# Expert feed-forward on one Trainium2 core: the low-input products of the last 64 features as two 64-row matmuls

## The chip, the cores and the metric

The kernel runs on one core of one Trainium2 chip. The metric is the device time in microseconds (us) of one execution, the median of several; a change is read against that median.

## The reference, cut to what matters

An image tokenizer and text tokens give 32 sequences of 164 tokens of width 192. An attention-like block follows, and then the part that this change touches, a feed-forward layer with 8 experts of width 384, of which each token uses 2:

```python
xn = _rms_norm(layernorm(h), norm_w)
xf = xn.reshape(-1, D)                      # D = 192
logits = xf @ router_w.T
probs = softmax(logits); _, top_idx = top_k(probs, 2)
g = einsum('td,efd->tef', xf, gate_w)       # 8 experts, 384 wide
u = einsum('td,efd->tef', xf, up_w)
h = silu(g) * u * comb_w[:, :, None]
y = einsum('tef,edf->td', h, down_w)
```

All is float32. The kernel reaches that accuracy with a faster matmul format: a value is split into a high part, which the format holds, and a low part, the remainder. A product of two values is then the sum of high by high, high by low and low by high.

## The kernel before, in words

The tokens are sorted by expert into tiles of 128 rows in DRAM (`disp`). The last stage works through 89 such tiles, called slots (`SLOTS = 89`), in a software pipeline with two of each buffer. Step k of the pipeline does on TensorE, in this order: "x", the two transposes of slot k+2 (L941); "g", gate's and up's matmuls of slot k+1 (L952 to L956); "h", the three transposes of the hidden tile of slot k (L963); "t", the six matmuls of the down projection of slot k-1 (L972, L974). ScalarE makes the high parts (`xh`, `hth`), the SiLU and a copy; VectorE makes the low parts (`xl`, `htl`), the product of gate and up (`hh`), and the sum of the result tile (`ysb`). GpSimd copies the 128 destination rows of the slot (`dnow`, L687) and issues the indirect DMA that scatters the result (L690). SP loads the next slot's rows (L428 to L431).

The weights stay in SBUF in `wa`, 128 partitions, per expert three blocks (r = 0, 1, 2) of 384 columns for gate and 384 for up. Block 0 holds the high parts of features 0 to 127, block 1 their low parts. Block 2, called rest, holds features 128 to 191, the high parts in partitions 0 to 63 and the low parts in partitions 64 to 127. The inputs `xh` and `xl` hold these 64 features twice, in both halves of their second 128 columns, so one 128-row matmul with rest gives the product with the high and the low part of the weight together. Each of gate and up therefore takes five matmuls of 128 rows by 384 columns: L952 (xh by high), L953 (xh by low), L954 (xl by high), L955 (xh by rest), L956 (xl by rest). The expert of a slot is read from a table (`tab`) into a register, and `wa` is addressed by that register. All ten matmuls end with one semaphore increment, on which ScalarE waits for the SiLU.

Earlier in the kernel, between patch tokens and the attention block, `text_kv` (L752) and `head_kv` (L760) issue pairs of float32 matmuls of 64 rows, one of partitions 0 to 63, the next of partitions 64 to 127, into different PSUM banks. A float32 matmul call there leaves two records in the trace, one after the other.

The weights' low parts are made on VectorE by `low`, in units spread over the attention loop; the low part of rest is made in partitions 64 to 127 for gate and for up.

Of the kernel before, what the change touches and what calls it, by code (L numbers as in the profile page):

```python
# [10 lines left out]
F32R = mybir.dt.float32r  # L11
# [4 lines left out]
P = 128  # L16
# [19 lines left out]
NE = 8  # L36
DE = 384
FC = DE // P
REGION = TILES * P + P
SLOTS = TILES * 2 + NE - 1  # L40
# [34 lines left out]
UNITS = DOWN_UNITS + 3 * NE  # L75
RING = 3
# [2 lines left out]
LN_GROUPS = (range(9, 17), range(17, 25), range(25, 33), range(33, 41), EARLY, LATE)  # L79
NORMED = tuple(t for g in LN_GROUPS for t in g)  # L80
XBUF = 3
TURNS = 2 * CHUNKS


# [23 lines left out]
def build(nc, pixels, bands, text, W, bias, attn_w, par, norm_w, router_w, gu_w, down_w, consts, out):  # L108
    with ExitStack() as ctx:
# [4 lines left out]
        def at(name, shape, dt, offset):  # L114
            return nc.alloc_sbuf_tensor_at(name, shape, dt, offset=offset)
# [13 lines left out]
        def sem(name):  # L129
            return ctx.enter_context(nc.semaphore(name))  # L130
# [5 lines left out]
        r_gh = room(2 * 2 * NH * D * 4)  # L136
# [16 lines left out]
        wa = at("wa", [P, NE * 3 * 2 * DE], F32R, r_w)  # L153
        wa5 = wa[:].rearrange("p (e r w f) -> p e r w f", e=NE, r=3, w=2)
        wd = at("wd", [P, NE * FC * 2 * D], F32R, r_wd)
        wd4 = wd[:].rearrange("p (g h d) -> p g h d", h=2, d=D)
        ring = [at(f"ring{i}", [P, DE], F32, r_gh + 18688 + 1536 * i) for i in range(RING)]
# [18 lines left out]
        xl = [at(f"xl{i}", [P, 2 * P], F32R, r_ffn + 2048 + 1024 * i) for i in range(2)]  # L176
# [3 lines left out]
        htl = [at(f"htl{i}", [P, DE], F32R, r_ffn + 13312 + 1536 * i) for i in range(2)]  # L180
        ysb = [at(f"ysb{i}", [P, D], F32, r_ffn + 16384 + 768 * i) for i in range(2)]
        ylo = [at(f"ylo{i}", [P, D], F32, r_ffn + 17920 + 768 * i) for i in range(2)]

        yall = at("yall", [P, TILES * 2 * D], F32, r_w)

# [2 lines left out]
        tab = sb("tab", [P, 2, TAB], I32)  # L188
# [19 lines left out]
        nwab = qpar[:, Q_NORM:Q_GB]  # L208
# [45 lines left out]
        bank = [ctx.enter_context(nc.psum_tensor(f"bank{i}", [P, 512], F32)) for i in range(5)]  # L254
# [38 lines left out]
        s_hi, s_lo, s_cnt = sem("expert_high"), sem("expert_low"), sem("counts_ready")  # L293
        s_cread, s_tab, s_zf = sem("counts_mm"), sem("table"), sem("tail_zeroed")
# [3 lines left out]
            "xsT_mm", "xsT_high", "xsT_low", "gate_up_mm", "silu", "hidden"))  # L298
        s_ht, s_hth, s_htl, s_dn, s_y = (sem(n) for n in (
            "hiddenT_mm", "hiddenT_high", "hiddenT_low", "down_mm", "y_ready"))  # L300
        s_ylo = sem("down_low_out")
        s_exp, s_w, s_dest, s_dnow = (sem(n) for n in (
            "softmax_exp", "weights_ready", "result_rows", "result_rows_copied"))
        s_yg = [sem(f"results_in{i}") for i in range(len(LOADS) - 1)]
# [353 lines left out]
        @block.gpsimd  # L658
        def _(pool):
            pool.memset(onesf[:], 1.0).then_inc(s_pool, 1)  # L660
            pool.memset(ident[:], 0.0).then_inc(s_pool, 1)
            pool.memset(onesb[:], 1.0).then_inc(s_pool, 1)
            pool.memset(ltri[:], 1.0).then_inc(s_pool, 1)
            pool.wait_ge(s_pool, 4)
            pool.affine_select(out=ident[:], in_=ident[:], compare_op=ALU.not_equal, fill=1.0, base=0,
                               pattern=[[-1, P]], channel_multiplier=1)

            pool.affine_select(out=ltri[:], in_=ltri[:], compare_op=ALU.is_gt, fill=0.0, base=0,
                               pattern=[[1, P]], channel_multiplier=-1).then_inc(s_cons, 1)


            def scatter(c):
                pool.wait_ge(s_pos, c + 1)
                for j in range(nt(c)):
                    pool.wait_ge(s_xf, 4 * c + j + 1)
                    pool.nop(nofuse=True)
                    for k in range(2):
                        pool.indirect_dma_start(disp, bass.IndirectOffsetOnAxis(  # L678
                            ap=posu[c % XBUF][:, 2 * j + k:2 * j + k + 1], axis=0), xfd[c % XBUF][:, j, :], None
                            ).then_inc(s_scat[c % XBUF][j], 16)  # L680

            for c in range(CHUNKS):
                scatter(c)

            def store(k, b):
                pool.wait_ge(s_y, k + 1)
                pool.tensor_copy(dnow[b][:], dest[:, bass.ds(k, 1)]).then_inc(s_dnow, 1)  # L687
                pool.wait_ge(s_dnow, k + 1)
                pool.nop(nofuse=True)
                pool.indirect_dma_start(ydram, bass.IndirectOffsetOnAxis(ap=dnow[b][:], axis=0),  # L690
                                        ysb[b][:], None).then_inc(s_ys[b], 16)

            with pool.Fori(0, SLOTS // 2) as i:
                for b in range(2):
                    store(2 * i + b, b)
            if SLOTS % 2:
                store(SLOTS - 1, 0)

        @block.tensor
        def _(pe):  # L700
# [232 lines left out]
            def step(k, b, parts="xght"):  # L933

                if "x" in parts:

                    pe.wait_ge(s_xs[b], 16 * (k - b + 4))
                    if not isinstance(k, int) or k >= -1:
                        pe.wait_ge(s_xlo, k + 2)
                    for m in range(2):  # L940
                        ins = pe.transpose(bank[5][:, P * m:P * m + P], xs[b][:, P * m:P * m + P], ident[:])  # L941
                    ins.then_inc(s_xst, 1)
                if "g" in parts:
                    o = 1 - b
                    e = pe.snap(gate_reg[o], min_val=0, max_val=NE - 1)
                    pe.wait_ge(s_xlo, k + 2)


                    for which in range(2):
                        high, low, rest = (wa[:, bass.ds(e * (6 * DE) + 2 * DE * r + DE * which, DE)] for r in range(3))  # L950
                        acc = bank[2 * o + which][:, 0:DE]
                        pe.matmul(acc, xh[o][:, 0:P], high, start=True, stop=False)  # L952
                        pe.matmul(acc, xh[o][:, 0:P], low, start=False, stop=False)  # L953
                        pe.matmul(acc, xl[o][:, 0:P], high, start=False, stop=False)  # L954
                        pe.matmul(acc, xh[o][:, P:2 * P], rest, start=False, stop=False)  # L955
                        ins = pe.matmul(acc, xl[o][:, P:2 * P], rest, start=False, stop=True)  # L956
                    ins.then_inc(s_gu, 1)
                if "h" in parts:
                    pe.wait_ge(s_hh, k + 1)
                    if not isinstance(k, int) or k >= 1:  # L960
                        pe.wait_ge(s_htl, k)
                    for c in range(FC):
                        ins = pe.transpose(bank[4][:, P * c:P * c + P], hh[b][:, P * c:P * c + P], ident[:])  # L963
                    ins.then_inc(s_ht, 1)
                if "t" in parts:
                    o = 1 - b
                    e = pe.snap(down_reg[o], min_val=0, max_val=NE - 1)
                    pe.wait_ge(s_htl, k)
                    for c in range(FC):
                        both = bass.ds(e * (FC * 2 * D) + c * 2 * D, 2 * D)  # L970
                        high = bass.ds(e * (FC * 2 * D) + c * 2 * D, D)
                        pe.matmul(bank[6 + o][:, 0:2 * D], hth[o][:, P * c:P * c + P], wd[:, both],  # L972
                                  start=(c == 0), stop=False)
                        ins = pe.matmul(bank[6 + o][:, 0:D], htl[o][:, P * c:P * c + P], wd[:, high],  # L974
                                        start=False, stop=(c == FC - 1))
                    ins.then_inc(s_dn, 1)
                if "g" in parts:
                    pe.reg_mov(down_reg[1 - b], gate_reg[1 - b])
                    if not isinstance(k, int) or k + 3 < TAB:
                        pe.reg_load(gate_reg[1 - b], tab[0:1, 1, bass.ds(k + 3, 1)])  # L980
# [4 lines left out]
        def _(v):  # L985
# [280 lines left out]
            def low(n):  # L1266
                v.wait_ge(s_hi, n + 1)
                if unit(n) is None:
                    raw = wd4[:, 6 * n:6 * n + 6, 1, :]
                    ins = v.tensor_tensor(raw, raw.bitcast(F32), wd4[:, 6 * n:6 * n + 6, 0, :].bitcast(F32), ALU.subtract)  # L1270
                else:
                    e, k = unit(n)
                    if k == 0:
                        raw = wa5[:, e, 1]
                        ins = v.scalar_tensor_tensor(out=raw, in0=raw.bitcast(F32), scalar=nwab[:, 0:1],
                                                     in1=wa5[:, e, 0].bitcast(F32), op0=ALU.mult, op1=ALU.subtract)
                    else:
                        both = wa5[64:P, e, 2, k - 1, :]
                        ins = v.scalar_tensor_tensor(out=both, in0=ring[(2 * e + k - 1) % RING][64:P, :], scalar=nwab[64:P, 1:2],
                                                     in1=both.bitcast(F32), op0=ALU.mult, op1=ALU.subtract)  # L1280
                ins.then_inc(s_lo, 1)

# [207 lines left out]
```

## Time and profile before

| what | value |
|---|---|
| median of 3 runs | 587.46 us (587.01 to 587.70) |
| the profiled execution's own time | 587.44 us |
| its span, first to last instruction | 585.7 us |
| mean granted TensorE clock | 0.916 of full |
| TensorE busy, share of the span | 83% |
| VectorE, ScalarE, GpSimd busy | 63%, 48%, 32% |
| matmuls L952 to L956 | 178 each: 89 slots, gate and up |

An execution takes a little longer than its span, because something lies ahead of the first and behind the last instruction. In the timeline, a matmul's record is longer than the time until the next one may start, since matmuls overlap in the array; what a matmul costs is read from start to start. "PEld" is the load of the stationary operand, which may run beside the matmul before.

### The profile page before, as it was taken

The page shows a single profiled execution, that of the slowest core. Times are in us where ns is not written, and L with a number is a line of the kernel's source. Part 1 is how long each engine was busy: PE and PEld are TensorE (multiplying, and loading weights), DVE is VectorE, ACT ScalarE, POOL GpSimd, SP SyncE. Part 2 cuts the span into 40 slices and gives each one's busy share as a digit, 9 for nine tenths or more (in the row PEclk, how much of TensorE's full clock was granted, in tenths as well). Part 3 has the DMA queues.
Part 4 walks back from the last instruction along what each step waited for, and adds up shares of the span by engine and source line. Part 5 has one row for each costly group of instructions (what it writes and reads, how often), then busy time and mean ns, then how long its engine had stood idle before and what let it go on. Part 6 is the DMA issues. An engine that isn't in the chain of part 4 may idle for free.

```text
span 585.7 us, 12736 instructions
## 1 busy us (share of the span) xinstructions
PE 486.6 (83%) x3132; PEld 458.1 (78%) x3133; DVE 367.7 (63%) x1263; ACT 281.5 (48%) x703; POOL 188.1 (32%) x270
## 2 busy tenths in 40 slices
PE   4999999996889896029999999999999999999000
PEld 2799999885777674029999999999999999999000
DVE  2648955245979889815556556556556656655397
ACT  0268944444868786514544544544544544544000
POOL 0000000003577777721333333333333333333200
PEclk9999999597989998559999999999999999999655
DMA  8993112810234333322222222222222222221597
GB/s 350 433 412 130 51 59 59 318 41 22 68 84 136 104 116 117 110 75 60 72 70 79 74 68 79 74 68 79 75 67 79 76 67 79 77 66 51 226 396 225
DMA packets 52027, 71.62 MB, mean 122 GB/s; under 512 B 18993, under 2 KB 45426, under 8 KB 50466
## 3 DMA queue, kind: packets, MB, share of 16 engines
q1 hardware_dynamic: 39632, 47.93, 25.8%
q0 software_dynamic: 8208, 16.95, 8.1%
q10 hardware_dynamic: 4162, 6.45, 3.0%
q8 instruction: 11, 0.18, 0.1%
q14 instruction: 14, 0.11, 0.1%
HBM read 49.43 MB, written 21.86 MB: 122 GB/s over the span
## 4 chain that ended last, share of the span: by engine, by line
PE 71%; DVE 19%; DMA 4%; issue 3%; POOL 2%; ACT 1%; SPq 0%; DVEq 0%; POOLq 0%; ACTq 0%
PE bank L722 7%; PE bank L956 5%; PE bank L954 5%; PE bank L952 5%; PE pair L722 5%; PE bank L953 5%; PE bank L955 5%; PE bank L963 5%; DVE hres L1375 4%; PE bank L972 4%; PE pair L972 4%; PE pair L941 4%; PE pair L858 3%; PE pair L862 2%; DVE stats L1210 2%
## 5 line engine op out<-in xcount | busy, mean ns | idle before, releaser
L678 POOL DMA_INDIRECT disp<-xf,posu x82 | 83.1, 1013 | 168.7 <-ACT xf L578 145.1
L690 POOL DMA_INDIRECT ydram<-ysb,dnow x89 | 87.3, 981 | 69.4 <-POOL dnow L687 67.2
L1350 DVE TENSOR_TENSOR hh<-sg,bank 128x384 f32<-128x384 f32 x89 | 49.4, 555 | 94.3 <-ACT sg L640 94.3
L640 ACT ACTIVATE sg<-bank 128x384 f32<-128x384 f32 x89 | 43.7, 491 | 114.7 <-PE bank L956 114.7
L952 PE MATMUL bank<-wa,xh 128*128 x178 | 67.8, 381 | 0.0
L956 PE MATMUL bank<-wa,xl 128*128 x178 | 60.5, 340 | 0.0
L954 PE MATMUL bank<-wa,xl 128*128 x178 | 60.4, 339 | 0.0
L953 PE MATMUL bank<-wa,xh 128*128 x178 | 60.2, 338 | 0.0
L955 PE MATMUL bank<-wa,xh 128*128 x178 | 60.0, 337 | 0.0
L687 POOL COPY dnow<-dest 128x1 uint32 (+1 forms) x89 | 16.3, 184 | 119.3 <-DVE ysb L1360 119.3
L941 PE MATMUL pair<-ident,xs 128*128 128x128 f32 x178 | 34.9, 278 | 21.4 <-DMA xs<-disp 20.4
L1353 DVE TENSOR_TENSOR htl<-bank,hth 128x384 fp32r<-128x384 f32 x89 | 49.0, 550 | 0.9 <-ACT hth L643 0.9
L972 PE MATMUL pair<-wd,hth 128*128 x135 | 44.4, 379 | 0.4 <-DVE htl L1353 0.4
L963 PE MATMUL bank<-ident,hh 128*128 128x128 f32 x267 | 43.5, 272 | 0.6 <-DVE htl L1353 0.6
L972 PE MATMUL bank<-wd,hth 128*128 x132 | 43.5, 380 | 0.0
L643 ACT CAST hth<-bank 128x384 fp32r<-128x384 f32 x89 | 42.2, 475 | 0.8 <-PE bank L963 0.8
L722 PE MATMUL bank<-wcT,imgT 128*128 128x193 f32 x240 | 40.2, 327 | 1.2 <-DVE zrow L1007 1.2
L722 PEld LDWEIGHTS bank<-wcT,imgT 128*128 128x128 f32 x240 | 39.3, 189 | 1.7 <-DVE zrow L1007 1.6
L637 ACT CAST xh<-pair 128x256 fp32r<-128x256 f32 x89 | 33.4, 375 | 11.1 <-PE pair L941 11.1
L858 PE MATMUL pair<-nst,xT 96*128 96x208 f32 x164 | 37.9, 355 | 0.6 <-DVE z L1205 0.6
L941 PEld LDWEIGHTS pair<-ident,xs 128*128 128x128 f32 x178 | 20.8, 143 | 21.9 <-DMA xs<-disp 21.8
L963 PEld LDWEIGHTS bank<-ident,hh 128*128 128x128 f32 x267 | 34.8, 141 | 3.6 <-DVE hh L1350 0.8
(232 smaller groups left out, 1151.8 us busy)
## 6 DMA issues: line engine op xcount, KB each, us to landing
xs<-disp SPq DMA_DIRECT2D x89, 96.0 KB, 2.0
imgT<-in_pixels SPq DMA_DIRECT2D x4, 1536.0 KB, 17.8
band<-in_bands SPq DMA_DIRECT2D x4, 1536.0 KB, 12.9
yall<-ydram ACTq DMA_DIRECT2D x5, 768.0 KB, 12.8
hres<-in_text SPq DMA_DIRECT2D x1, 3072.0 KB, 34.0
wa<-in_gate_up_w SPq DMA_DIRECT2D x8, 384.0 KB, 8.4
ring<-in_gate_up_w SPq DMA_DIRECT2D x32, 96.0 KB
yall<-ydram SPq DMA_DIRECT2D x4, 768.0 KB, 13.8
```

The costliest lines, as they stand in the source:

```text
L678: pool.indirect_dma_start(disp, bass.IndirectOffsetOnAxis(ap=posu[c % XBUF][:, 2 * j + k:2 * j + k + 1], axis=0), xfd[c % XBUF][:, j, :], None
L690: pool.indirect_dma_start(ydram, bass.IndirectOffsetOnAxis(ap=dnow[b][:], axis=0), ysb[b][:], None).then_inc(s_ys[b], 16)
L722: ins = pe.matmul(bank[PATCH_BANK[p % 4]][:, 0:193], imgT[:, 2 * i + dr, j + s, c, :], wcT[:, k, :], start=(k == 0), stop=(k == 23))
L858: pe.matmul(o, xT[c % 2][:, m, P * j:P * j + P], nst[c % 2][:, m, :], start=(m == 0), stop=False)
L941: ins = pe.transpose(bank[5][:, P * m:P * m + P], xs[b][:, P * m:P * m + P], ident[:])
L952: pe.matmul(acc, xh[o][:, 0:P], high, start=True, stop=False)
L953: pe.matmul(acc, xh[o][:, 0:P], low, start=False, stop=False)
L954: pe.matmul(acc, xl[o][:, 0:P], high, start=False, stop=False)
L955: pe.matmul(acc, xh[o][:, P:2 * P], rest, start=False, stop=False)
L956: ins = pe.matmul(acc, xl[o][:, P:2 * P], rest, start=False, stop=True)
L963: ins = pe.transpose(bank[4][:, P * c:P * c + P], hh[b][:, P * c:P * c + P], ident[:])
L972: pe.matmul(bank[6 + o][:, 0:2 * D], hth[o][:, P * c:P * c + P], wd[:, both], start=(c == 0), stop=False)
```

## The change

The ten matmuls of gate and up become eight of 128 rows and two of 64 rows. L956 (xl by rest, 128 rows) goes, for gate and for up. Behind the other eight stand two matmuls of 64 rows: gate's takes xl's partitions 0 to 63 and the weights' high part in partitions 0 to 63, up's takes partitions 64 to 127 of both. To have up's high part in partitions 64 to 127, `low` now leaves it there and makes the low part in partitions 0 to 63. The product of low input and low weight of these features is no longer computed. Up's matmul reads its weights from one of two fixed buffers `upr`, which GpSimd fills from `wa` with a copy of 128 x 384 float32 for each slot, four slots ahead of the slot whose result it stores.

```diff
+AHEAD = 4
...
+        upr = [at(f"upr{i}", [P, DE], F32R, r_gh + 6144 + 1536 * i) for i in range(2)]
...
-            with pool.Fori(0, SLOTS // 2) as i:
+            def fetch(s, b):
+                if not isinstance(s, int) or s >= 2:
+                    pool.wait_ge(s_gu, s - 1)
+                e = pool.value_load(tab[0:1, 1, bass.ds(s, 1)], min_val=0, max_val=NE - 1)
+                pool.tensor_copy(upr[b][:], wa[:, bass.ds(e * (6 * DE) + 5 * DE, DE)]).then_inc(s_upr, 1)
+
+            pool.wait_ge(s_lo, UNITS)
+            pool.wait_ge(s_tab, 1)
+            for s in range(AHEAD):
+                fetch(s, s % 2)
+            n = (SLOTS - AHEAD) // 2
+            with pool.Fori(0, n) as i:
                 for b in range(2):
+                    fetch(2 * i + (AHEAD + b), b)
                     store(2 * i + b, b)
-            if SLOTS % 2:
-                store(SLOTS - 1, 0)
+            for k in range(2 * n, SLOTS):
+                if k + AHEAD < SLOTS:
+                    fetch(k + AHEAD, k % 2)
+                store(k, k % 2)
...
                     pe.wait_ge(s_xlo, k + 2)
+                    pe.wait_ge(s_upr, k + 2)
                     for which in range(2):
...
                         pe.matmul(acc, xh[o][:, P:2 * P], rest, start=False, stop=False)
-                        ins = pe.matmul(acc, xl[o][:, P:2 * P], rest, start=False, stop=True)
+                    for which in range(2):
+                        a = 64 * which
+                        rest = upr[o][a:a + 64, :] if which else wa[0:64, bass.ds(e * (6 * DE) + 4 * DE, DE)]
+                        ins = pe.matmul(bank[2 * o + which][:, 0:DE], xl[o][a:a + 64, P:2 * P], rest, start=False, stop=True)
                     ins.then_inc(s_gu, 1)
...
-                        both = wa5[64:P, e, 2, k - 1, :]
-                        ins = v.scalar_tensor_tensor(out=both, in0=ring[(2 * e + k - 1) % RING][64:P, :], scalar=nwab[64:P, 1:2],
+                        half = slice(64, P) if k == 1 else slice(0, 64)
+                        both = wa5[half, e, 2, k - 1, :]
+                        ins = v.scalar_tensor_tensor(out=both, in0=ring[(2 * e + k - 1) % RING][half, :], scalar=nwab[half, 1:2],
                                                      in1=both.bitcast(F32), op0=ALU.mult, op1=ALU.subtract)
```

## Rows read from the trace of the kernel before

**Rows 1.** The page's granted TensorE clock, in 40 slices of the span, in tenths.
```profile
PEclk9999999597989998559999999999999999999655
```

**Rows 2.** Busy time by stretch: length, then PE, PEld, DVE, ACT, POOL, clock.
```profile
300.00:400.00 100.00, 100.00 (x672) 98.97 (x671) 60.23 (x160) 47.87 (x128) 37.24 (x64) 1.00 0.26 74
```

**Rows 3.** Groups by line: count, busy us and mean ns, idle before.
```profile
L956 PE MATMUL bank<-wa,xl 128*128 x178 | 60.5, 340 | 0.0
```

**Rows 4.** Timeline (start us, length us), TensorE, one slot of the loop.
```profile
401.75 0.38 PE L941 MATMUL pair<-ident,xs 128*128 128x128 f32 x2
401.89 0.42 PE L952 MATMUL bank<-wa,xh 128*128 x1
402.15 0.34 PE L953 MATMUL bank<-wa,xh 128*128 x1
...
403.36 0.33 PE L955 MATMUL bank<-wa,xh 128*128 x1
403.54 0.34 PE L956 MATMUL bank<-wa,xl 128*128 x1
403.71 0.49 PE L963 MATMUL bank<-ident,hh 128*128 128x128 f32 x3
...
404.87 0.38 PE L941 MATMUL pair<-ident,xs 128*128 128x128 f32 x2
```

**Rows 5.** Timeline, weight loads of the same slot.
```profile
401.86 0.19 PEld L952 LDWEIGHTS bank<-wa,xh 128*128 128x128 f32 x1
...
401.97 0.19 PEld L953 LDWEIGHTS bank<-wa,xh 128*128 128x128 f32 x1
...
403.54 0.42 PEld L963 LDWEIGHTS bank<-ident,hh 128*128 128x128 f32 x3
```

**Rows 6.** Timeline, TensorE, from 128-row matmuls (L722) to 64-row pairs (L752).
```profile
96.71 0.98 PE L722 MATMUL bank<-wcT,imgT 128*128 128x193 f32 x5
97.62 0.35 PE L752 MATMUL bank<-k0T,aw 64*96 64x128 f32 x1
97.63 0.35 PE L752 MATMUL pair<-k0T,aw 64*96 64x128 f32 x1
97.81 0.27 PE L752 MATMUL bank<-k0T,aw 64*96 64x128 f32 x1
...
97.92 0.27 PE L752 MATMUL bank<-k0T,aw 64*96 64x128 f32 x1
```

**Rows 7.** Timeline, the weight load at the same switch.
```profile
97.62 0.16 PEld L752 LDWEIGHTS bank<-k0T,aw 64*96 64x96 f32 x1 [0.23 <-issue]
```

**Rows 8.** Timeline, TensorE, from 64-row pairs (L752) to 128-row matmuls (L802).
```profile
100.00 0.27 PE L752 MATMUL pair<-k0T,aw 64*96 64x128 f32 x1
...
100.11 0.27 PE L752 MATMUL pair<-k0T,aw 64*96 64x128 f32 x1
...
100.31 0.35 PE L802 MATMUL bank<-selr,onesf 128*96 128x24 f32 x2
```

**Rows 9.** Timeline, from pairs to L825, which waits for nothing, at half clock.
```profile
113.59 0.42 PE L752 MATMUL bank<-v0T,aw 64*96 64x128 f32 x1
113.79 0.42 PE L752 MATMUL pair<-v0T,aw 64*96 64x128 f32 x1
113.80 0.42 PE L752 MATMUL bank<-v0T,aw 64*96 64x128 f32 x1
114.15 0.66 PE L825 MATMUL bank<-x0T,qpar 96*128 96x176 f32 x1
```

**Rows 10.** Timeline, VectorE and GpSimd, one slot of the loop.
```profile
402.47 0.36 DVE L1360 TENSOR_TENSOR ysb<-pair,ylo 128x192 f32<-128x192 f32 x1
402.99 0.18 POOL L687 COPY dnow<-dest 128x1 uint32 x1 [1.21 <-DVE ysb L1360]
403.94 0.98 POOL L690 DMA_INDIRECT ydram<-ysb,dnow  x1 [0.76 <-POOL dnow L687]
```

**Rows 11.** GpSimd's widest operation, at the start of the kernel.
```profile
1.65 0.28 POOL L665 TENSOR_SCALAR_AFFINE_SELECT ident<-ident 128x128 f32<-128x128 f32 x1 [0.24 <-POOL ltri L663]
```

**Rows 12.** Chain of waits before the loop: last scatter, SP's table read and load.
```profile
252.94 2.42 DMA disp<-xf,posu
255.73 0.27 SPq L428
256.47 0.37 SPq L429
```

**Rows 13.** Timeline, the first gate matmul of the loop.
```profile
260.94 0.67 PE L952 MATMUL bank<-wa,xh 128*128 x1
```

More of the change, by code:

```diff
@@ L300, in build @@
             "hiddenT_mm", "hiddenT_high", "hiddenT_low", "down_mm", "y_ready"))
-        s_ylo = sem("down_low_out")
+        s_ylo, s_upr = sem("down_low_out"), sem("up_rest_fetched")
         s_exp, s_w, s_dest, s_dnow = (sem(n) for n in (
```

## The prediction

> **What bounds the kernel now.** I read the slices of the page first, then the busy times by stretch, then the groups by line, then one slot of the timeline engine by engine, and last the chain of waits at the loop's start. The 89 slots, from 261 us on [rows 13], take 3.12 us each [rows 4], 278 us or nearly half of the time. There TensorE bounds: in the 100 us from 300 to 400 it is busy for all 100.00 us at a clock of 1.00, beside 60 us on VectorE, 48 on ScalarE and 37 on GpSimd [rows 2]. The clock stays at nine tenths or more in every slice of the loop's body [rows 1]. L956, whose matmuls the change takes out, never has idle time before it [rows 3]. Busy time is not cost, though: its mean record is 340 ns [rows 3], but from its start to the next instruction's it takes 403.71 - 403.54 = 0.17 us, as does the L955 before it (0.18) [rows 4]. I use 0.173, the spacing over the ten matmuls. A whole slot takes 404.87 - 401.75 = 3.12 us [rows 4]. So whatever is added to or taken from TensorE's sequence per slot counts 89 times, as long as no other engine becomes later.
>
> **The change part by part.**
>
> *Removed and added matmuls.* Per slot two 128-row matmuls go and a pair of 64-row ones comes. The 64-row pairs of before really do run side by side: the second starts 0.01 us after the first (97.62, 97.63), and the next pair starts 97.92 - 97.81 = 0.11 us later [rows 6]. They are float32 with 128 columns, where ours are the fast format with 384; I let ours take one matmul's 0.173 plus 0.01. The work itself therefore shrinks by 0.163 us per slot, 14.5 us in 89.
>
> *Going into 64-row matmuls.* This is the term that decides. Within the loop, the weights of the next matmul are loaded during the one before: L963's load begins at 403.54, together with the last L956 and 0.17 us ahead of its own matmul, although L963 also has a semaphore to wait for [rows 5, 4]. At the switch to 64 rows that is not so. The five L722 records start (0.98 - 0.33)/4 = 0.163 us apart, so the last starts at 97.36; the first 64-row matmul starts at 97.62, 0.26 later instead of 0.163 [rows 6]. Its weight load starts at the same 97.62, behind 0.23 us in which the loader waited for nothing shown [rows 7]. The switch costs 0.10 us (0.094 unrounded), in which the array empties. Then the load, no longer hidden, delays the pair: the second pair comes 0.19 us after the first instead of 0.107 [rows 6], 0.083 for 96 columns; ours load 128, in proportion 0.11. The loop shows the same for an open load of 128 columns: L952's load at 401.86, L953's at 401.97, and L953 0.26 instead of 0.173 after L952 [rows 5, 4].
>
> *Coming back.* From the last pair at 100.11 to the next 128-row matmul at 100.31 are 0.20 us instead of 0.107 [rows 8]: 0.093. That place has a semaphore wait in the code, so I looked for one without: L825 follows the pairs with no wait at all and starts 0.35 us behind the last one, where pairs are 0.21 apart, at half clock [rows 9], 0.14 more. The switch itself costs then, not the wait. L963's first weight load, today hidden [rows 5], comes into the open: again 0.11.
>
> The sum per slot: 0.094 + 0.11 + 0.093 + 0.11 = 0.407 added, 0.163 removed, +0.244. Times 89: +21.7 us. Bounds: if neither switch nor open load costs anything, -0.163 per slot or -14.5 us; if each switch costs the 0.14 of the half-clock row [rows 9], +0.337 or +30 us. I take the fast-clock rows, because the loop runs at full clock [rows 2]. For the open loads the low bound is the 0.083 of 96 columns [rows 6], which makes +17 us.
>
> The Trainium skill, TensorEngine Tiling (Array Packing), Key Properties, says that changing the tiling mode, and not merely the tile, drains TensorE. The trace agrees, with the 0.09 to 0.10 us of [rows 6, 8]. The page gives no price for the drain.
>
> *GpSimd's copy.* Per slot GpSimd gets a wait, a register load, and a copy of 128 x 384. Today it starts dnow at 402.99 and is free at 403.94 + 0.98 = 404.92, 1.93 us later, and idles 1.21 us for ysb [rows 10]. No row shows such a copy. From below: dnow's 0.18 for one column and the 0.28 of the widest operation, 128 columns [rows 10, 11], give 0.8 ns a column and 0.48 us for 384. From above: 0.28 per 128 columns all in, 0.85. The nearest row for the register load is SP's, 0.27 for the load alone and 256.47 - 255.73 = 0.74 until the value is used [rows 12]. A fetch is then 0.75 to 1.59 us; I take 0.74 + 0.48 = 1.2, the copy by the slope because a start is paid once. GpSimd's turn becomes 1.93 + 1.2 = 3.1 us. It fits into 3.12 + 0.24 = 3.36 us and costs nothing; it would not have fitted into 2.96. The fetch stands ahead of store, so store and ysb's two buffers wait behind it, and behind the gate wait of slot k+2. That gate ends in the middle of pipeline step k+1, while the result that store waits for comes from the same step's end, so the wait holds nothing up. The new wait on TensorE, in front of the gate matmuls, has x and the whole rest of the slot queued behind it; the copy for slot k+4 is made about a slot before it is needed, so it passes.
>
> *At the loop's start* GpSimd is free behind the last scatter, which starts at 252.94 and by [rows 10] holds it for 0.98 us; the copy of slot 0 needs about 1.2 us from some 254 us, and the first gate matmul starts at 260.94 [rows 12, 13]. SP's load is the longer chain. Nothing.
>
> *VectorE's low* works on 64 partitions as before, only on the other half for up. Nothing. The output wait, the final loads and stores do not move.
>
> Sum against the profiled execution: its own time is 587.44 us, span 585.7, and the median of the runs shown is 587.46, so both starts agree. 587.4 + 21.7 = 609.1 us.
>
> **The rivals.**
>
> *A. The pair is as good as it looks (faster).* The f32 rows are no guide for the fast format, or the queue hides the switch because it is filled far ahead in the loop. The slot then loses 0.163 us: 587.4 - 14.5 = 573 us. For it: the side-by-side starts of [rows 6]. Against it: in every switch of the trace the load starts only with its matmul [rows 7], with a filled queue too. It decides as soon as the two switches and two open loads together cost under 0.163 us per slot, against the 0.407 above; and GpSimd's fetch must stay under 2.96 - 1.93 = 1.03 us.
>
> By the Trainium skill, TensorE: Matmul & The Clock Gate, Part 3, packed tiles span one matmul plus some 4 ns for each further one; that alone would make the slot 0.169 us shorter and the time about 572 us. The trace agrees on the side-by-side start (10 ns) but that formula has no term for going in and out.
>
> *B. The gain is there but GpSimd takes it (no change).* With A's TensorE and a fetch of 1.2 us, the slot is held at 1.93 + 1.2 = 3.13 us: 587 us or so.
>
> *C. GpSimd becomes the bound above TensorE (slower still).* With the fetch at its upper bound, 1.59 us, the slot takes 3.52 us, 0.40 more than now: +35.6 us, 623 us. It decides from a fetch of 3.36 - 1.93 = 1.43 us. For it: the copy reads and writes SBUF while VectorE works, and no row shows its rate. Against it: the slope of [rows 10, 11].
>
> *D. Half the cost.* The open loads are mostly absorbed: 0.187 of drains less 0.163, +0.024 per slot, 589.5 us, up to 600 if one of the two loads stays open.
>
> **How the numbers follow.** Forecast as summed, with its own range 601 to 617 (0.083 for the loads and slightly less drain at one end, half-clock drains at the other): 0.56. D: 0.10. C, 617 to 625 and beyond: 0.13. A: 0.14. B: 0.07; half of it lies a little to a side. A measurement of this kernel tells about 0.2%, 1.2 us, from no change. Faster: A and a little of B, 0.15. Same: most of B, 0.06. Slower: the rest, 0.79. Below 583 lies nearly all of A, above 621 about a third of C; the range is 583 to 621.
>
> **What would show each step.** In the profile after, inside a slot: the two 64-row matmuls start within about 0.01 us of each other; their weight loads start with them and not during the last L955; the first of them comes 0.26 to 0.28 us behind that matmul; L963 comes about 0.38 us behind the pair instead of 0.17, with its load at the same instant. The slot takes 3.33 to 3.40 us, TensorE's listed idle time stays near nothing, the clock stays 1.00, and GpSimd still idles for ysb, 0.1 to 0.4 us. The prediction is wrong if the loads are pulled ahead across the switch, if the slot is below 3.12 us, or if TensorE stands idle for upr or VectorE for a stored result, which would be C.

## The result

| | median us | runs | lowest to highest |
|---|---|---|---|
| before | 587.58 | 4 | 587.01 to 588.39 |
| changed | 606.43 | 4 | 604.05 to 607.83 |

The ratio on record is 1.0303, 95% interval 1.0276 to 1.0329; the quotient of the two medians, 1.0321, lies inside it. By the medians the change makes the kernel 18.85 us slower. The forecast was 609.1, within 583 to 621.

The slot is the quantity to compare. I take it from the starts of the result DMAs, one per slot, between about 300 and 500 us of one profiled execution: 63 steps in 197.40 us before, 3.133 us each (the 3.12 of [rows 4] is one slot; short and long ones alternate). After, the first and the last in that stretch are 60 slots apart, 3.328 us each (timeline of the changed kernel, GpSimd; start, length, instruction):

```profile
299.97 0.98 POOL L693 DMA_INDIRECT ydram<-ysb,dnow  x1 [0.76 <-POOL dnow L690]
...
499.67 0.98 POOL L693 DMA_INDIRECT ydram<-ysb,dnow  x1 [0.76 <-POOL dnow L690]
```

That is +0.195 us per slot, 17.4 us in 89. In the profiled execution, which at 607.83 us is the longest of the four, the first gate matmul comes 3.36 us later (264.30 against 260.94 [rows 13]); the work ahead of the loop differs from run to run by some us and is no part of the edit that I can name.

Beside each series of experiments the kernel before was run again and scattered between 613 and 628 us; a ratio leaves out runs more than 1.5% above the fastest of the same kernel (five of its seven beside e1 to e4), while a difference of medians takes them all.

### The profile page after: what moved, and what is told of

Its sections match the earlier page's. It is cut to its first block, busy times and chain, and to the rows that moved or that the text cites. A ratio compares the mean times of both kernels' runs of the same rounds, so it can differ in the third digit from the quotient of the medians.

```text
span 606.1 us, 13428 instructions
## 1 busy us (share of the span) xinstructions
PE 504.3 (83%) x3132; PEld 440.3 (73%) x3133; DVE 367.7 (61%) x1263; ACT 289.3 (48%) x703; POOL 235.5 (39%) x360
## 4 chain that ended last, share of the span: by engine, by line
PE 71%; DVE 18%; DMA 4%; issue 3%; POOL 2%; ACT 1%; POOLq 0%; SPq 0%; DVEq 0%; ACTq 0%
PE bank L982 7%; PE bank L739 7%; PE bank L975 5%; PE bank L971 5%; PE bank L968 5%; PE bank L970 5%; PE bank L969 5%; PE pair L739 5%; PE pair L991 4%; DVE hres L1395 4%; PE bank L991 4%; PE pair L958 3%; PE pair L875 3%; PE pair L879 2%; PE pair L993 2%
## 5 line engine op out<-in xcount | busy, mean ns | idle before, releaser
L681 POOL DMA_INDIRECT disp<-xf,posu x82 | 84.7, 1033 | 170.1 <-ACT xf L581 146.2
L968 PE MATMUL bank<-wa,xh 128*128 x178 | 68.4, 384 | 0.0
L971 PE MATMUL bank<-wa,xh 128*128 x178 | 61.1, 343 | 0.0
L970 PE MATMUL bank<-wa,xl 128*128 x178 | 60.8, 341 | 0.0
L969 PE MATMUL bank<-wa,xh 128*128 x178 | 60.4, 339 | 0.0
L700 POOL CAST upr<-wa 128x384 fp32r x89 | 45.7, 514 | 15.7 <-PE bank L975 15.2
L982 PE MATMUL bank<-ident,hh 128*128 128x128 f32 x267 | 48.7, 291 | 0.4 <-DVE htl L1373 0.4
L991 PE MATMUL pair<-wd,hth 128*128 x135 | 45.1, 383 | 0.4 <-DVE htl L1373 0.4
L991 PE MATMUL bank<-wd,hth 128*128 x132 | 43.5, 379 | 0.0
L982 PEld LDWEIGHTS bank<-ident,hh 128*128 128x128 f32 x267 | 27.6, 140 | 16.9 <-issue 16.3
L975 PE MATMUL bank<-wa,xl 64*128 x89 | 39.5, 444 | 0.0
L975 PE MATMUL bank<-upr,xl 64*128 64x384 f32 x89 | 39.1, 439 | 0.0
```

The costliest lines, as they stand in the source:

```text
L681: pool.indirect_dma_start(disp, bass.IndirectOffsetOnAxis(ap=posu[c % XBUF][:, 2 * j + k:2 * j + k + 1], axis=0), xfd[c % XBUF][:, j, :], None
L975: ins = pe.matmul(bank[2 * o + which][:, 0:DE], xl[o][a:a + 64, P:2 * P], rest, start=False, stop=True)
```

## The profile after

The same view as [rows 4], one slot of the changed kernel on TensorE:

```profile
301.11 0.38 PE L958 MATMUL pair<-ident,xs 128*128 128x128 f32 x2
301.25 0.42 PE L968 MATMUL bank<-wa,xh 128*128 x1
...
302.39 0.33 PE L970 MATMUL bank<-wa,xl 128*128 x1
302.57 0.34 PE L971 MATMUL bank<-wa,xh 128*128 x1
302.84 0.44 PE L975 MATMUL bank<-wa,xl 64*128 x1
302.84 0.44 PE L975 MATMUL bank<-upr,xl 64*128 64x384 f32 x1
303.21 0.55 PE L982 MATMUL bank<-ident,hh 128*128 128x128 f32 x3
303.51 0.42 PE L991 MATMUL bank<-wd,hth 128*128 x1
...
304.43 0.39 PE L958 MATMUL pair<-ident,xs 128*128 128x128 f32 x2
```

And its weight loads, against [rows 5]:

```profile
302.83 0.18 PEld L975 LDWEIGHTS bank<-wa,xl 64*128 64x128 f32 x1 [0.25 <-issue]
302.84 0.18 PEld L975 LDWEIGHTS bank<-upr,xl 64*128 64x128 f32 x1
303.21 0.31 PEld L982 LDWEIGHTS bank<-ident,hh 128*128 128x128 f32 x3 [0.18 <-issue]
303.49 0.19 PEld L991 LDWEIGHTS bank<-wd,hth 128*128 128x128 f32 x1
```

The two 64-row matmuls start in the same hundredth of a microsecond. But the weight load of each block starts only with its matmul, where L963's load used to run 0.17 us ahead. In front of both loads the loader stands idle (0.25 and 0.18 us) for nothing that the profile can name. From the last 128-row matmul to the pair are 0.27 us, from the pair to the transposes 0.37, and from there to the down projection 0.30. None of these gaps shows as idle time of TensorE, because a matmul's modelled record covers it (0.34 us of record over the 0.27, 0.44 over the 0.37): in the stretch of [rows 2] it is as busy as ever, with fewer instructions (672 before).

```profile
300.00:400.00 100.00, 100.00 (x633) 86.92 (x634) 57.11 (x150) 47.70 (x121) 50.53 (x91) 1.00 0.25 69
```

PEld's 86.92 us (98.97 before) is the view that tells: the loader now has holes. The clock is still 1.00.

GpSimd, the same view as [rows 10]:

```profile
300.96 0.51 POOL L700 CAST upr<-wa 128x384 fp32r x1
302.35 0.19 POOL L690 COPY dnow<-dest 128x1 uint32 x1 [0.88 <-DVE ysb L1380]
303.30 0.98 POOL L693 DMA_INDIRECT ydram<-ysb,dnow  x1 [0.76 <-POOL dnow L690]
```

The copy takes 0.51 us and starts in the instant at which the DMA instruction ends (299.97 + 0.98 = 300.95); the wait and the register load (0.29 us by the median, on GpSimd's sequencer, while the DMA instruction runs) add nothing. GpSimd still idles 0.88 us per slot.

## The experiments

They ran in three series on three chips (e1 to e4, e5 to e8, e9 and e10); which chip the two kernels above ran on is not on record. In these series the kernel before takes 621 to 625 us by the median, 34 to 38 us more than above. Where a trace can be set beside the kernel before, the extra time is ahead of the loop: in e2, whose TensorE work is that of before, the first gate matmul starts at 296.22 us instead of 260.94. The chain of waits of e2 has eight pieces there, of 0.6 to 5.1 us and 26 us together, which the profile can put down to nothing in the kernel; the chain of the kernel before has none. The longest is

```profile
192.58 5.13 another core or an unknown queue
```

The theories are told apart by slots, and the medians stand beside them as differences from the kernel before of the same series. Each slot comes from one profiled execution; the granted clock is 1.00 from 310 to 500 us in all of them. The kernel before itself was not profiled again, but e1 (the changed kernel's TensorE work without the copy) and e2 (before's with the copy) each read 0.002 to 0.003 us more than their counterpart: a copy that cost time would move the two apart, so neither copy nor series moves the slot by more. What is left comes from one step near the loop's start (3.49 us in e1), which in the experiments falls into the stretch; their slots read up to 0.003 us high by it. By their ratios e1 to e4 leave the verdict at 2% unclear, so these four are read by their slots.

Theory T: going from the whole array to 64-row tiles and back empties the array and leaves a weight load in the open, twice per slot. Rivals: C, GpSimd's copy or its waits; S, the 64-row matmul itself is slow; O, the pair doesn't overlap; R, any matmul with fewer rows pays. In the table the differences are taken before rounding.

| kernel | slot us | against 3.133 | x 89 | median less before's |
|---|---|---|---|---|
| changed | 3.328 | +0.195 | +17.4 | +18.9 |
| e1, no copy | 3.330 | +0.197 | +17.5 | +20.0 |
| e2, copy only | 3.136 | +0.002 | +0.2 | -1.4 |
| e3, pair first | 3.359 | +0.226 | +20.1 | +18.5 |
| e4, split | 3.890 | +0.756 | +67.3 | +64.7 |
| e5, pair twice | 3.476 | +0.342 | +30.5 | +29.4 |
| e6, no pair | 2.793 | -0.341 | -30.3 | -31.3 |
| e7, gate's alone | 3.331 | +0.198 | +17.6 | +19.2 |
| e8, every other slot | 3.140 | +0.006 | +0.6 | +0.5 |
| e9, 96 rows | 3.156 | +0.023 | +2.0 | -1.0 |
| e10, same half | 3.476 | +0.343 | +30.5 | +27.2 |

**e1, no copy in the loop.**

```diff
-            for s in range(AHEAD):
+            for s in range(2):
                 fetch(s, s % 2)
...
-                    fetch(2 * i + (AHEAD + b), b)
...
-                    pe.wait_ge(s_upr, k + 2)
+                    pe.wait_ge(s_upr, 2)
```

> The changed kernel without GpSimd's copy per slot: two copies at the start, none in the loop, and TensorE waits for these two only (so up's 64-row matmul reads the weights of the first slots' expert). T, the switches and open loads on TensorE cost the time: slot 3.33 us, time 605 to 607, as the changed kernel. Rival C, GpSimd's copy or its waits slow the others: slot towards 3.13 us, time 588 to 600.

Ratio 1.0443 (1.0268 to 1.0618). The slot stays at 3.330 us. The copy costs nothing; C falls.

**e2, the copy alone.**

```diff
                         pe.matmul(acc, xh[o][:, P:2 * P], rest, start=False, stop=False)
+                        ins = pe.matmul(acc, xl[o][:, P:2 * P], rest, start=False, stop=True)
-                    for which in range(2):
-                        a = 64 * which
...
```

> All ten matmuls with 128 rows as before, but GpSimd's copy per slot and TensorE's wait for it kept (the weights keep the changed layout, with up's high part in the upper half). T: slot 3.13 us, time 587 to 588, no different from before. Rival C: 595 or more.

The ratio, 1.0128 (0.9977 to 1.028), can't tell 2%; the slot can: 3.136 us. With e1 this clears GpSimd from both sides.

**e3, the pair ahead of the eight.** The pair is issued before the loop over the eight.

```diff
+                    for which in range(2):
+                        a = 64 * which
+                        rest = upr[o][a:a + 64, :] if which else wa[0:64, bass.ds(e * (6 * DE) + 4 * DE, DE)]
+                        pe.matmul(bank[2 * o + which][:, 0:DE], xl[o][a:a + 64, P:2 * P], rest, start=True, stop=False)
                     for which in range(2):
...
-                        pe.matmul(acc, xh[o][:, 0:P], high, start=True, stop=False)
+                        pe.matmul(acc, xh[o][:, 0:P], high, start=False, stop=False)
...
```

> The changed kernel with the 64-row pair ahead of the eight 128-row matmuls. T: the same two switches, so L941 to L953 grows from 0.40 to about 0.89 us, the last 128-row matmul to the hidden transposes shrinks from 0.64 to 0.17, and the transposes' first load is hidden again (-0.05): slot 3.30 us, time 602 to 605. Rival (the place behind the eight is at fault, because the pair waits for them in the same banks): slot near 2.97, time 573 to 580.

Ratio 1.042 (1.0261 to 1.0579), slot 3.359 us, 0.03 more than the changed kernel where I had expected 0.03 less. Timeline of e3, TensorE:

```profile
322.37 0.38 PE L958 MATMUL pair<-ident,xs 128*128 128x128 f32 x2
322.68 0.44 PE L968 MATMUL bank<-wa,xl 64*128 x1
...
323.06 0.44 PE L972 MATMUL bank<-wa,xh 128*128 x1
...
323.34 0.34 PE L973 MATMUL bank<-wa,xh 128*128 x1
```

The back half came as expected (its last matmul to the transposes 321.04 to 321.21, and 0.25 on to L991). The front did not. From the first of the two short transposes to the pair are 0.31 us, where I had put 0.23: without a switch the first gate matmul follows at 0.14 (301.11 and 301.25 in the changed kernel), so this way in costs 0.17 and not 0.094. Why it is dearer here, no run shows. The rival (the place behind the eight) falls: the price is paid in either place.

**e4, split.**

```diff
                         pe.matmul(acc, xh[o][:, P:2 * P], rest, start=False, stop=False)
-                    for which in range(2):
                         a = 64 * which
-                        rest = upr[o][a:a + 64, :] if which else wa[0:64, bass.ds(e * (6 * DE) + 4 * DE, DE)]
-                        ins = pe.matmul(bank[2 * o + which][:, 0:DE], xl[o][a:a + 64, P:2 * P], rest, start=False, stop=True)
+                        half = upr[o][a:a + 64, :] if which else wa[0:64, bass.ds(e * (6 * DE) + 4 * DE, DE)]
+                        ins = pe.matmul(acc, xl[o][a:a + 64, P:2 * P], half, start=False, stop=True)
```

> Each 64-row matmul directly behind its own four 128-row ones, so no pair and four switches per slot. T: one more excursion of 0.094 + 0.11 + 0.173 + 0.093 + 0.087 = 0.56 us: slot 3.88 us, time 654. Rival S, the 64-row matmul itself is slow (half rate, 0.33 us) and switches are free: slot 3.33 + 0.33 - 0.01 = 3.65, time 633.

Ratio 1.1117 (1.0723 to 1.1512). 3.890 against T's 3.88 and S's 3.65: one further excursion costs 0.56 us. The loader shows it four times in a slot; the first two, in the timeline of e4:

```profile
320.86 0.34 PE L971 MATMUL bank<-wa,xh 128*128 x1
321.13 0.18 PEld L974 LDWEIGHTS bank<-wa,xl 64*128 64x128 f32 x1 [0.25 <-issue]
321.13 0.44 PE L974 MATMUL bank<-wa,xl 64*128 x1
321.50 0.19 PEld L968 LDWEIGHTS bank<-wa,xh 128*128 128x128 f32 x1 [0.18 <-issue]
321.50 0.44 PE L968 MATMUL bank<-wa,xh 128*128 x1
```

A single 64-row matmul has the very gaps of the pair, 0.27 and 0.37. This first one is gate's, in the lower half and with its weights from `wa`, so neither `upr` nor the upper half makes them.

**e5, the pair twice.**

```diff
-                    for which in range(2):
+                    for n in range(4):
+                        which = n % 2
...
```

> The changed kernel with the 64-row pair issued twice in a row (its product is added twice). T, a pair streams as fast as one 128-row matmul and the price is in going in and out: +0.18 us, slot 3.51 us, 34 us above before. Rival S, the pair itself is slow (half rate): +0.33 us, slot 3.66 us, 47 us above before.

Ratio 1.0557 (1.0478 to 1.0636). The second pair adds 3.476 - 3.328 = 0.148 us to the slot, half of what S asks for: S falls. TensorE in e5:

```profile
331.52 0.34 PE L971 MATMUL bank<-wa,xh 128*128 x1
331.79 0.44 PE L976 MATMUL bank<-wa,xl 64*128 x1
331.79 0.44 PE L976 MATMUL bank<-upr,xl 64*128 64x384 f32 x1
332.07 0.34 PE L976 MATMUL bank<-wa,xl 64*128 x1
332.07 0.34 PE L976 MATMUL bank<-upr,xl 64*128 64x384 f32 x1
332.34 0.55 PE L983 MATMUL bank<-ident,hh 128*128 128x128 f32 x3
```

Pair to pair 0.28 us: the first pair's open load and its 384 columns. Pair to transposes 0.27, the second pair's load hidden now: the columns and the emptying, the same 0.27 as on the way in. The single pair of the changed kernel, with its load in the open, has 0.37 there: the open load is worth 0.10. Between the last 128-row matmul and the transposes e5 takes 332.34 - 331.52 = 0.82 us and the changed kernel 303.21 - 302.57 = 0.64, so the second pair itself takes 0.18, as long as a 128-row matmul. The other 0.03 is time that e5's slot is shorter elsewhere, most of it in the eight matmuls (first to last start 1.30 us instead of 1.32); why, no run shows.

**e6, no pair.** The 64-row matmuls are left out, and with them the low input by high weight of the last 64 features.

```diff
-                        pe.matmul(acc, xh[o][:, P:2 * P], rest, start=False, stop=False)
+                        ins = pe.matmul(acc, xh[o][:, P:2 * P], rest, start=False, stop=True)
-                    for which in range(2):
-                        a = 64 * which
...
```

> The changed kernel with no 64-row matmuls (low input by high weight of the last 64 features is left out); the copy stays. T: 3.13 less two 128-row matmuls of 0.173: slot 2.79 us, 31 us below before, so the pair's whole price is 0.54 us per slot. If GpSimd's turn with the copy (3.1 us in the prediction) were real, the slot would stop at 3.1 us; the trace of the changed kernel suggests 2.6 us, which would not show.

Ratio 0.9545 (0.947 to 0.962). The slot is 2.793 us. So the pair's whole excursion costs 3.328 - 2.793 = 0.535 us, where the two 128-row matmuls that it replaced cost 3.133 - 2.793 = 0.340. GpSimd, with its copy, still keeps up (timeline of e6):

```profile
331.86 0.51 POOL L700 CAST upr<-wa 128x384 fp32r x1
332.71 0.19 POOL L690 COPY dnow<-dest 128x1 uint32 x1 [0.34 <-DVE ysb L1376]
```

**e7, gate's 64-row matmul alone.** Up's is left out.

```diff
...
-                    for which in range(2):
-                        a = 64 * which
...
+                    ins = pe.matmul(bank[2 * o][:, 0:DE], xl[o][0:64, P:2 * P], wa[0:64, bass.ds(e * (6 * DE) + 4 * DE, DE)],
+                                    start=False, stop=True)
```

> The changed kernel with gate's 64-row matmul only (up's is left out). T, the second of the pair is free: slot 3.32 us, 17 us above before. Rival O, the two do not really overlap: 0.16 us less, slot 3.16 us, about as before.

Ratio 1.0367 (1.0258 to 1.0477). 3.331 us with one, 3.328 with both: the second of the pair is free, O falls. What the change set out to do, it does.

**e8, the pair twice in every other slot.**

```diff
...
-                    for which in range(2):
+                    for n in range(4 * b):
+                        which = n % 2
...
```

> The pair twice in every other slot and not at all in the others (so the same number of 64-row matmuls as the change, half the switches; the product is doubled in one slot and missing in the next). T: per two slots 2 x 2.79 + 0.54 + 0.18 = 6.30 us, slot 3.15 us, 1 to 2 us above before: sharing one excursion between two slots would only win back what was lost. Rival S: per two slots 5.57 + 0.54 + 0.33, slot 3.22, 8 us above before.

Ratio 1.0055 (1.0005 to 1.0105), slot 3.140. Half the switches for the same 64-row work win back what was lost and no more. As a real kernel, which would need the next slot's low input a step earlier, it was not tried: with two slots to an excursion its best case is the time of before.

**e9, two matmuls of 96 rows.**

```diff
...
+                        rest = wa[0:96, bass.ds(e * (6 * DE) + 4 * DE + DE * which, DE)]
+                        ins = pe.matmul(bank[2 * o + which][:, 0:DE], xl[o][0:96, P:2 * P], rest, start=False, stop=True)
```

> Instead of the 64-row pair two matmuls of 96 rows, one after the other, both from the register-addressed weights (their product is not the one wanted). Whole-array matmuls with idle rows. T, it is the change between 64-row tiles and the whole array that costs: no open weight load and no gap, slot 3.13 us, as before (0 to 1 us). Rival R, any matmul that uses fewer rows than its neighbour pays: slot 3.3 us or more, 15 us above before.

Ratio 0.9984 (0.995 to 1.0019), slot 3.156 (0.02 above T, far from R's 3.3). Fewer rows as such cost next to nothing, and the loads are pulled ahead again, as this stretch of e9 shows:

```profile
331.30 0.33 PE L971 MATMUL bank<-wa,xh 128*128 x1
331.30 0.36 PEld L974 LDWEIGHTS bank<-wa,xl 96*128 96x128 f32 x2
331.47 0.51 PE L974 MATMUL bank<-wa,xl 96*128 x2
331.65 0.43 PEld L981 LDWEIGHTS bank<-ident,hh 128*128 128x128 f32 x3
331.82 0.49 PE L981 MATMUL bank<-ident,hh 128*128 128x128 f32 x3
```

**e10, both 64-row matmuls in the lower half.**

```diff
...
+                        rest = wa[0:64, bass.ds(e * (6 * DE) + 4 * DE + DE * which, DE)]
+                        ins = pe.matmul(bank[2 * o + which][:, 0:DE], xl[o][0:64, P:2 * P], rest, start=False, stop=True)
```

> Both 64-row matmuls in partitions 0 to 63 (up's product is not the one wanted). T, the two overlap only because they use different halves of the array: one excursion as in the changed kernel plus 0.15 to 0.17 us for the second, slot 3.48 to 3.49 us, 32 us above before. Rival, matmuls in 64-row mode into different banks overlap anyway: slot 3.33 us.

Ratio 1.0463 (1.039 to 1.0535). 3.476 us, 0.148 above the changed kernel: two in the same half run one after the other, two in different halves together.

No experiment gives a version that beats both kernels and computes what the reference asks for. By these numbers one excursion for three slots would win, as an estimate 3 x 0.340 - (0.535 + 2 x 0.148) = 0.19 us in three slots, some 6 us in all; it would need low inputs and accumulators of three slots at once, where the kernel has two of each, and was not tried.

## Why the prediction was right

*The bound.* TensorE set the slot before and sets it after; no other engine's wait grew into it (e1 and e2 for GpSimd, and TensorE's 100.00 us busy of 100).

*The work saved.* Put at 0.163 us per slot, with 0.173 for each matmul and 0.01 for the pair's offset. The offset is nothing (e7), the two matmuls taken out were worth 0.340 together (e6), and a pair takes 0.18 where its load is hidden (e5). The saving was 0.16, as written.

*Going in.* 0.094 for the emptying and 0.11 for the open load. The changed kernel has 0.27 us from the last 128-row matmul to the pair, where 0.267 was written, and pair to pair takes 0.28 in e5, where 0.173 and 0.11 make 0.283. Both terms stand. That [rows 6] are of another format and of 96 columns did not matter.

*Coming back.* 0.093 for the emptying: 0.37 us from the pair to the transposes, against 0.376. It stands. The last term failed in size: the open load of the first transpose was put at 0.11, and the stretch from the transposes to the down projection grew only from 0.25 to 0.30, by 0.05. Its end before, in the timeline of the slot of [rows 4], where L963 starts at 403.71:

```profile
403.96 0.42 PE L972 MATMUL bank<-wd,hth 128*128 x1
```

The records of the three transposes together are longer by that much, 0.55 us instead of the 0.49 of [rows 4]. The reason I read from the loads and did not test: that stretch was short of load time before too, three loads for little matmul work, so one more in the open replaces part of a wait that was there. With 0.05 in the place of 0.11 the sum is 0.347 - 0.163 = +0.184.

The trace shows that the sum closes. Means of start to start over the slots between 300 and 520 us:

| stretch, us | before | changed | difference | forecast |
|---|---|---|---|---|
| first transpose of x to first gate matmul | 0.138 | 0.140 | +0.002 | 0 |
| from there to the first hidden transpose | 1.836 | 1.962 | +0.126 | +0.134 |
| from there to the down projection | 0.245 | 0.303 | +0.058 | +0.11 |
| from there to the next slot | 0.915 | 0.923 | +0.008 | 0 |

The second row holds the removed and added matmuls, both switches and the pair's open load. So the one term that was mis-sized is the open load of the transposes, 0.058 instead of 0.11; the rest was right to 0.01 each.

*In sum* +21.7 us was forecast and 18.85 measured: 17.4 in the slots, and 1.5 outside them, where the forecast had nothing and no run shows a cause.

*GpSimd's copy.* Cost nothing, as forecast, but by more than the working said: a fetch of 1.2 us was taken, and it is 0.51. The slope's 0.48 was nearly right; SP's 0.74 for the register load was the wrong row, since on GpSimd that runs beside the DMA instruction. GpSimd idles 0.88 us for ysb where 0.1 to 0.4 was written. The turn is 0.19 + 0.76 + 0.98 + 0.51 = 2.44 us instead of 3.1. Rival B (GpSimd takes the gain) was therefore never possible: e6 runs at 2.79 us with the copy. Rival C asked for a fetch of 1.43 us and had no ground either.

*Rival A* was right on the pair and wrong on the way in and out. The overlap that the Trainium skill, TensorE: Matmul & The Clock Gate, Part 3, describes is here to the hundredth (302.84 and 302.84). What decided is the way in and out. The Trainium skill, TensorEngine Tiling (Array Packing), Key Properties, says that changing the tiling mode drains TensorE; the trace agrees, with [0.25 <-issue] and [0.18 <-issue] before the two loads, and so does e9, whose 96-row matmuls have neither. The drain is a little more than half of what the way in and out costs, 0.10 and 0.09 us; the open loads are 0.10 and 0.058.

## What to carry to other kernels

Price a 64-row pair as an excursion, not as one matmul: here 0.535 us for one pair of 384 columns, then 0.148 for each further pair, against 0.17 per whole-array matmul. As an estimate from these numbers it needs three pairs in a row (0.535 + 2 x 0.148 = 0.83 against 6 x 0.17 = 1.02) to win, and two only break even; two are measured (e8), three are not. When TensorE's busy share is 100%, look at the weight loader's row too: here its busy time fell from 98.97 to 86.92 us in 100, and the loads that start with their matmul and not before it mark where the time went.

## What the runs showed that I had not expected

- The way in is not a constant: it adds 0.10 us behind a matmul of 384 columns (0.27 instead of 0.17 from start to start), but 0.17 behind the two short transposes (0.31 instead of 0.14 from the first of them, e3). Why stays open.
- GpSimd's register load and semaphore wait cost nothing behind an indirect DMA instruction; a 128 x 384 float32 copy takes 0.51 us and slows neither TensorE (e2, 3.136 us a slot) nor VectorE (its product `hh` takes 554 ns in the changed kernel and took 555).
- The kernel before took 34 to 38 us more in the three series of experiments than in the first measurement. In e2's trace the first gate matmul is 35.28 us later, and 26 us of its chain of waits ahead of it are pauses that no engine or queue of the kernel accounts for. What they are stays open.
